# A transformer block pair with routed experts: three scatters under way at a time, copies under the first attention, the second stack loaded sooner

## The reference

```
x = x + attention_a(layernorm(x))      # 16 heads of 16, causal, K.Q scores with a distance decay
x = x + experts(layernorm(x))
x = x + attention_b(layernorm(x))      # 16 heads of 16, causal, Q.K scores
x = x + experts(layernorm(x))

experts(flat):                         # flat: 4096 x 256
  shared = sum over 2 of relu(flat @ sw1 + sb1) @ sw2 + sb2, divided by 2     # hidden 176
  probs  = softmax(flat @ router_w + router_b)                                # 32 experts
  top 6 of the 32 per token, their probabilities divided by their sum = gates
  routed = sum over 32 of gate * (relu(flat @ w1 + b1) @ w2 + b2)             # hidden 176
  return shared + routed
```

## Time and profile before

| | us |
|---|---|
| median of 3 runs | 3484.1 (3482.74 to 3485.52) |
| profiled execution, its own time | 3493.54 |
| profiled execution, span from first to last instruction | 3491.3 |
| mean granted TensorE clock | 0.881 of full speed |
| busy share: PE, DVE, ACT, POOL | 76%, 60%, 47%, 40% |

### The profile page before, as it was taken

One profiled execution on the slowest core, in us unless ns is written; L12 is line 12 of the kernel. 1 busy time (PEld: TensorE's weight loads), 2 busy tenths in 40 slices (PEclk: granted clock), 3 DMA queues, 4 the chain that ended last, 5 costly groups with the idle time before them and its releaser, 6 DMA issues.

```text
span 3491.3 us, 71965 instructions
## 1 busy us (share of the span) xinstructions
PE 2659.0 (76%) x17832; PEld 1972.4 (56%) x17832; DVE 2082.1 (60%) x4604; ACT 1640.8 (47%) x2861; POOL 1402.4 (40%) x1058
## 2 busy tenths in 40 slices
PE   7599984967935699999384999849579346899982
PEld 6355553534524588888372555535345235888882
DVE  8466662745523378888493666636455234777772
ACT  3145441423501288888340454314235003888882
POOL 3410013031054188888545000230400451888885
PEclk9799996978967799999797999879789668999996
DMA  9865442453444489888858744524534435898888
GB/s 329 188 131 101 79 117 81 91 148 91 128 163 151 155 154 156 153 154 155 175 193 165 133 90 90 122 73 89 149 83 142 173 139 163 153 156 151 153 155 196
DMA packets 317212, 494.50 MB, mean 142 GB/s; under 512 B 55659, under 2 KB 225005, under 8 KB 311725
## 3 DMA queue, kind: packets, MB, share of 16 engines
q1 hardware_dynamic: 224844, 361.85, 40.0%
q0 software_dynamic: 92160, 130.08, 22.0%
HBM read 264.26 MB, written 256.77 MB: 149 GB/s over the span
## 4 chain that ended last, share of the span: by engine, by line
PE 45%; issue 16%; DMA 11%; another core or an unknown queue 10%; DVE 8%; POOL 4%; DVEq 2%; SPq 1%; ACT 1%; POOLq 1%; ACTq 0%
PE ps L1524 10%; PE ps L1538 10%; PE ps L1555 9%; DMA expert_sum<-x,route_u 7%; PE ps L1805 3%; DMA split<-rows_scratch 3%; PE ps L1542 2%; PE ps L1528 2%; POOL expert_sum L1439 2%; PE ps L1823 2%; DVE split L1128 2%; PE ps L1726 1%; PE ps L1600 1%; PE ps L1715 1%
## 5 line engine op out<-in xcount | busy, mean ns | idle before, releaser
L1239 ACT ACTIVATE work<-ps 128x1024 f32<-128x1024 f32 (+3 forms) x768 | 594.2, 809 | 926.7 <-PE ps L1542 468.8
L791 DVE TENSOR_REDUCE small<-ps 128x1 f32<-128x512 f32 (+3 forms) x1216 | 730.2, 657 | 462.8 <-PE ps L1528 185.0
L1439 POOL DMA_INDIRECT expert_sum<-x,route_u x512 | 829.8, 1621 | 210.3 <-issue 98.8
L1524 PE MATMUL ps<-split 128*128 128x512 f32 (+3 forms) x1536 | 527.3, 418 | 311.1 <-DVE small L791 156.0
L1405 POOL DMA_INDIRECT expert_rows<-x x288 | 277.9, 965 | 1099.5 <-DVE x L945 991.8
L1524 PEld LDWEIGHTS ps<-split 128*128 128x128 f32 x1536 | 283.8, 205 | 516.3 <-DVE small L791 305.8
L1538 PE MATMUL ps<-split 128*128 128x512 f32 (+3 forms) x1536 | 508.6, 411 | 8.9 <-DMA split<-split 8.0
L1805 PE MATMUL ps<-split 128*88 128x256 f32 x3072 | 417.2, 285 | 92.8 <-DVE split L1128 61.8
L1805 PEld LDWEIGHTS ps<-split 128*88 128x88 f32 x3072 | 363.0, 155 | 140.5 <-issue 136.4
L1823 PE MATMUL ps<-split 97*128 97x256 f32 x3072 | 408.9, 282 | 2.2 <-DVE split L1143 2.0
L1823 PEld LDWEIGHTS ps<-split 97*128 97x128 f32 x3072 | 384.7, 189 | 2.8 <-issue 2.8
(11 more groups left out here) (178 smaller groups left out, 3223.3 us busy)
## 6 DMA issues: line engine op xcount, KB each, us to landing
x<-expert_rows SPq DMA_DIRECT2D x256, 320.0 KB
split<-qks_scratch SPq DMA_DIRECT2D x192, 256.0 KB
qks_scratch<-split SPq DMA_DIRECT2D x64, 512.0 KB, 5.0
expert_rows<-in_pads SPq DMA_DIRECT2D x65, 320.0 KB, 29.9
v_scratch<-work SPq DMA_DIRECT2D x64, 256.0 KB, 4.4
split<-v_scratch SPq DMA_DIRECT2D x32, 512.0 KB, 14.0
xT_scratch<-split SPq DMA_DIRECT2D x16, 1024.0 KB, 11.9
split<-xT_scratch SPq DMA_DIRECT2D x16, 1024.0 KB
```

The source lines that it names most:

```text
L791: v.tensor_reduce(cols[:, heads[0]:heads[0] + len(heads), i], ps[:, task_bank(n), 0:w * len(heads)].rearrange("p (h k) -> p h k", k=w), AX ...
L1239: c.activation(pexp[:, (s % 2) * 2 + h, :, BLK - w:], ps[:, 2 * h:2 * h + 2, BLK - w:], ACT.Exp).then_inc(s_pe, 1)
L1439: pool.indirect_dma_start(acc[r], bass.IndirectOffsetOnAxis(ap=idx[:, j, k:k + 1], axis=0), ye[:, r3, k, :], None, compute_op=ALU.add).the ...
L1524: last = mm(bank[:, e, :], stack[:, r, 0, h, i * P:i * P + P], stack[:, r, 1, h, first:first + w], start=e == 0, stop=not diagonal and e = ...
```

## The change

`dispatch` gets three semaphores for each half of a batch instead of one, and before a scatter POOL waits until the one three before it has landed (`AHEAD = 3`). The other places that waited for a whole half now wait for three counts of 16 (`PER`) scatters. The copies of the second expert weights to scratch are cut into four pieces that SyncE issues in units 0 to 3 of the first attention, those of shared weights, pads and zeros in unit 4, and the wait for them moves from unit 0 to unit 15. The second stack is cleared, and its rows and stack are loaded, in phase 0, between the stores of the last two blocks; the third follows at the start of phase 1, ahead of the values of units 1 and 2. Tiles of 256 rows are in both kernels.

```
+AHEAD = 3
+PER = TPB * TOPK // AHEAD
...
-        s_disp = [sem(f"rows_dispatched{r}") for r in range(2)]
+        s_disp = [[sem(f"rows_dispatched{r}{c}") for c in range(AHEAD)] for r in range(2)]
...
                 if L == 0:
                     sp.dma_start(rows_scratch, a["rows"]).then_inc(s_rowc, 16)
-                    sp.dma_start(w2d, a["w2r"]).then_inc(s_init, 16)
-                    sp.dma_start(wsd, a["wsh"]).then_inc(s_init, 16)
-                    sp.dma_start(rows[0:TT], a["pads"]).then_inc(s_init, 16)
-                    for i in range(2):
-                        sp.dma_start(acc[i][NTOK:NTOK + TT].rearrange("(j p) d -> p j d", p=P),
-                                     a["zeros"].unsqueeze(1).broadcast_to([P, TJ, D])).then_inc(s_init, 16)
...
                 load_stack(0, 0)
-                store_batch(B - 1)
+                store_block(B - 1, 0)
+                load_rows(1)
+                load_stack(1, 1)
+                store_block(B - 1, 1)
                 phase_end(sp, L, 0)
...
                 load_neg_max(0)
                 load_values(0, 0)
+                load_rows(2)
+                load_stack(2, 2)
                 for r in (1, 2):
-                    load_rows(r)
-                    load_stack(r, r)
                     load_values(r, r)
...
                     if u == 0:
-                        sp.wait_ge(s_init, 80)
                         sp.wait_ge(s_bod, (L + 1) * NT)
                         sp.dma_start(xd.rearrange("(t p) d -> p t d", p=P), xv).then_inc(s_xst, 16)
+                    if L == 0 and u < 4:
+                        sp.dma_start(w2d[8 * u:8 * u + 8], a["w2r"][8 * u:8 * u + 8]).then_inc(s_init, 16)
+                    if L == 0 and u == 4:
+                        sp.dma_start(wsd, a["wsh"]).then_inc(s_init, 16)
+                        sp.dma_start(rows[0:TT], a["pads"]).then_inc(s_init, 16)
...
+                    if L == 0 and u == NU - 1:
+                        sp.wait_ge(s_init, 128)
...
                 for r in range(2):
-                    sp.wait_ge(s_disp[r], (L + 1) * (NBLK // 2 * TPB * TOPK * 16))
-                    apart(sp)
+                    for c in range(AHEAD):
+                        sp.wait_ge(s_disp[r][c], (L + 1) * (NBLK // 2 * PER * 16))
+                        apart(sp)
...
+                pool.wait_ge(s_pj, (L + 1) * (NBLK * 6))
+                pool.wait_ge(s_pl, (L + 1) * (NBLK * 4) + 4)
+                apart(pool)
+                for o in range(2):
+                    p.memset(stack32[64:P, 1, o], 0.0).then_inc(s_zero[1], 1)
                 phase_end(pool, L, 0)
...
                 def dispatch(b):
                     pool.wait_ge(s_pos, L * B + b + 1)
+                    if b:
+                        for c in range(AHEAD):
+                            pool.wait_ge(s_disp[1][c], (L * B + b) * (PER * 16))
                     apart(pool)
                     for t in range(2 * TPB):
                         for k in range(TOPK):
+                            n = t * TOPK + k
+                            if n >= AHEAD:
+                                r, m = divmod(n - AHEAD, TPB * TOPK)
+                                pool.wait_ge(s_disp[r][m % AHEAD], ((L * B + b) * PER + m // AHEAD + 1) * 16)
+                                apart(pool)
                             pool.indirect_dma_start(
                                 rows, bass.IndirectOffsetOnAxis(ap=posu[b][:, t * 8 + k:t * 8 + k + 1], axis=0),
-                                rowb[b][:, t // TPB, t % TPB, :], None).then_inc(s_disp[t // TPB], 16)
+                                rowb[b][:, t // TPB, t % TPB, :], None).then_inc(s_disp[t // TPB][n % AHEAD], 16)
```

More of the change, by code:

```diff
@@ L444, in _ @@
                 with sp.Fori(0, B - 1) as b:
-                    store_batch(b)
+                    for r in range(2):
+                        store_block(b, r)
                 sp.wait_ge(s_rowc, 16)
@@ L510, in _ @@
                     if u == 0:
-                        sp.wait_ge(s_init, 80)
                         sp.wait_ge(s_bod, (L + 1) * NT)
                         sp.dma_start(xd.rearrange("(t p) d -> p t d", p=P), xv).then_inc(s_xst, 16)
+                    if L == 0 and u < 4:
[3 more added lines that the diff above has]
+                        sp.dma_start(rows[0:TT], a["pads"]).then_inc(s_init, 16)
+                        for i in range(2):
+                            sp.dma_start(acc[i][NTOK:NTOK + TT].rearrange("(j p) d -> p j d", p=P),
+                                         a["zeros"].unsqueeze(1).broadcast_to([P, TJ, D])).then_inc(s_init, 16)
+                    if L == 0 and u == NU - 1:
+                        sp.wait_ge(s_init, 128)
                     for e in range(2 * u, 2 * u + 2):
@@ L856, in normalise_rows @@
                     if 0 < b < B - 1:
-                        dve.wait_ge(s_disp[r], (L * B + b) * (TPB * TOPK * 16))
-                        apart(dve)
+                        for c in range(AHEAD):
+                            dve.wait_ge(s_disp[r][c], (L * B + b) * (PER * 16))
+                            apart(dve)
                     for j in range(TPB):
@@ L1383, in _ @@
                     qk_lo(B - 1, r)
-                phase_end(pool, L, 0)
-                for r in (1, 2):
-                    if r == 2:
-                        for s in range(2):
-                            pool.wait_ge(s_pd[s], (L * B + B) * 64 + 64)
-                        apart(pool)
-                    for o in range(2):
-                        p.memset(stack32[64:P, r, o], 0.0).then_inc(s_zero[r], 1)
+                pool.wait_ge(s_pj, (L + 1) * (NBLK * 6))
[3 more added lines that the diff above has]
+                    p.memset(stack32[64:P, 1, o], 0.0).then_inc(s_zero[1], 1)
+                phase_end(pool, L, 0)
+                for s in range(2):
+                    pool.wait_ge(s_pd[s], (L * B + B) * 64 + 64)
+                apart(pool)
+                for o in range(2):
+                    p.memset(stack32[64:P, 2, o], 0.0).then_inc(s_zero[2], 1)
                 pool.wait_ge(s_bo, L * 16 + 16)
```

30 lines of the change are left out of this document (15 added, 15 removed).

## The result

| | before | after |
|---|---|---|
| median of the runs | 3484.8 us (3482.7 to 3487.7, 4 runs) | 3318.9 us (3315.9 to 3319.1, 4 runs) |
| span of the profiled execution | 3491.3 us | 3317.3 us |

The ratio is 0.952, with an interval of 0.9505 to 0.9538. The change is worth 166 us, where 405 were forecast. The profiled spans lie 174 us apart, and the two traces, cut where the last engine of each phase is through, say where: phase 0 is longer by 9 us over both layers, attention shorter by 66, phase 2 by 94, phase 3 by 22. Phase 0 and attention hold the second stack's gain and the stall's together.

A forecast was written before the change was run, and what follows sets the result against it. Bound: stalls while POOL issues scatters. 220 - 4 (attention) + 160 (phase 2) + 34 (second stack) - 5 (copies) = 405 us off 3484.1 gives 3079, written 3080 us; range 3025 to 3350.

The forecast's parts named there:

- What bounds the kernel: Attention and phase 2: PE, ACT and DVE stall while POOL issues a dispatch's 48 scatters; eight dispatches cost about their length.
- Dispatch, in attention: Four attention intervals with a dispatch: stall gone, 98.6 us becomes 44, gain 220 us (0 to 228).
- Rival C: Dispatches: the stall lasts as long as the train and the wait lengthens it, 3546 us; chance 0.07.
- The landing of 2.1 us: Dispatch: a scatter's data have moved 2.1 us after its start, so waiting for the one three back costs POOL little.
- Phase 2, 160 us: Phase 2: PE and DVE end 88 us sooner, dispatches become the path; 80 us a layer, 160 in all.
- the length of the trains: Phase 2: a dispatch's 48 scatters take 60.7 us, plus 3 for the slow start.
- Second stack, 34: Phase 0 into attention: unit 0 no longer waits for the second stack; 17 us per layer, 34 in all.
- Copies, -5: Attention, unit 0: the copies moved there hold SyncE's queue, costing 5 us (0 to 8).
- B: Dispatches: a limit of three hardly binds and the stall stays, 3479 us, or 3455; chance 0.11.
- P: Dispatches: part of the stall stays while SyncE's loads slow scatters, about 20 us per train, 3240 us; chance 0.12.

The follow-up runs named there:

- 3087 us: Changed kernel without its limit, a small POOL write behind every second scatter in attention's dispatches, every third in phase 2's: 3087.3 us (0.8833).
- the run with 1.63 us and no limit: Kernel before, no limit, one small POOL write, waited for, behind every second scatter of attention's dispatches: 3265.7 us (0.934).
- the bursts: Kernel before, no limit, POOL's pauses gathered behind each 8 or 24 scatters of attention's dispatches: 3372.6 us (0.9675) and 3455.4 us (0.990).

## Why the prediction was wrong

- **What bounds the kernel: right.** The stall in POOL's trains is what costs, and it can be had back: 3087 us was reached.
- **Dispatch, in attention, 220 us: wrong, the step that failed.** The step is the inference from the earlier trace rows that fewer scatters under way end the stall, so that a limit of three takes it away whole. Measured 25 us by the intervals, 19 to 29 by the runs. I read "48 given out, four in phase 3" as "the number given out and not the traffic". The comparison with the earlier trace rows had two differences, number and pace. 156 stores in 300 us are one each 1.9 us, against 1.26 in a dispatch, and the run with 1.63 us and no limit shows that the pace decides. My own text had what was needed: it said that "the wait costs POOL little". A wait that costs POOL nothing leaves the pace at 1.26, and so the stall. Rival C even had the rule, landing divided by the limit, but only as a danger and not as the cure.
- **The landing of 2.1 us** was read from the moved bytes. The release comes later: 3.28 us from start to start with one under way, where the bytes have moved after about 2 us too. By the Trainium skill ("Perfetto Trace Analysis", section "DMA Instruction — SWDGE (GPSIMD)") the last descriptor raises the semaphore only after the write before it is confirmed; no row here shows that step by itself. With 3.28 the rule is: pace = the larger of 1.26 and 3.28 / limit, so 1.26, 1.64 and 3.28 us for three, two and one; measured where no load is in the way are 1.26, 1.65 and 3.28.
- **Phase 2, 160 us: direction right, size wrong.** Measured 94. PE and DVE came free 98 us sooner, more than the 88 forecast. Here the same limit helped, since SyncE's loads hold the scatters and waits of 3 to 5 us break the train behind 3 to 10 scatters, 4 to 13 us of issuing; in the longer of these stretches "remote" waits of 3 to 4.4 us are left. That is read from the traces, with the bursts as support. The term that failed is the length of the trains: forecast 60.7 + 3, measured 87.6 and 72.5 us, and behind them a drain of 9.5 us for the 7.2 forecast.
- **Second stack, 34: right.** Unit 0's maxima at 158.25 (forecast 157), unit 1's at 195.54 (193 to 195); 16 us a layer in the traces, 29 us with the copies in the run without a limit.
- **Copies, -5: nothing.** The intervals of units 0 to 3 stayed at 37.3 us.
- **Phase 3, not in the sum: 22 us.** It takes 525 and 528 us before and 515 and 516 after. In layer 0 it was also shorter, by 5 to 10 us, in the runs in which PE and DVE were through long before POOL in phase 2. That its first loads then meet free queues is argued, not shown.
- **The rivals.** B said that a limit of three hardly binds and POOL issues every 1.26 us. In attention that is what happened, at a chance of 0.11; its price was wrong for phase 2, where the limit and what follows are worth 111 us. P put the stall in the first 20 us of a train; in the changed kernel PE is busy for nearly all of the first 24 us (490 to 514) and stands still later. C did not occur, though with one under way its mechanism did: the chain waited for a train of 193 us.
- **The range.** 3318.9 us lies within 3025 to 3350, but by luck: that end of the range was made for P, whose mechanism didn't occur. The 405 us are 220 - 4 for the attention where 25 came, 160 for phase 2 where 94 came, 34 for the stack where 32 came, -5 for the copies where nothing came, and nothing for phase 3 where 22 came; but for rounding these are the 174 us between the two traces.
- **A misreading.** The stall was said to end about 3 us behind the last scatter. DVE comes free at 573.01, 6 us behind that scatter's start and 5 behind its end. PE had written what DVE waits for 21 us before, at 552.16; it starts nothing more before 573.76:
```profile
551.36 0.80 PE L1524 MATMUL ps<-split 128*128 128x512 f32 x1 [12.50 <-issue]
```

## What to carry to other kernels

When an engine's stream of indirect DMAs stalls the others, find by runs the pace at which the stall goes, and give the DMAs out no faster. A limit on how many are under way does that only if the landing, read from the release of a waiting instruction, divided by the limit is as long as that pace (here 3.28 / 2 = 1.64 is, 3.28 / 3 = 1.09 isn't even as long as the engine's own step). Before a comparison with a healthy phase is used as a reason, list all that differs: here number and pace went together, and a run that changes one of them costs little.

## What the hardware showed that I had not expected

- Indirect stores of 128 rows of 1280 bytes given out each 1.26 us stop PE, ACT and DVE almost wholly after some 7 to 11 us, though what they wait for was written up to 21 us before (56.3 us lost in a train); at a mean of 1.63 us they cost nothing, at 1.50 us 11 us, at 1.44 us 31. In phase 3 stores of another kind, each 1.9 us, cost nothing either.
- The scatters themselves are not late in the stall: in the changed kernel each from 522 us on found the one three before it, 3.8 us old, landed, while ACT waited 29.82 us. Which resource holds the other engines stays open; a scatter with fewer rows or shorter ones, which would tell descriptors from instructions, wasn't tried.
- A direct copy of 164 KB on POOL's queue behind each scatter stretched the train from 119 to 181 us (two scatters under way in both, each copy waiting for the one before); SyncE's copies of 2 MB a unit cost neither the train (76.8 us, 76.6 without them) nor the engines anything.
